# Keys kept once in the first stage, and experts' rows scattered straight to their tokens: one core of Trainium2

## The reference, cut to what matters

```
x = x + xattn0(layernorm(x), ctx)      # layer 0: 8 batches x 16 heads, 256 queries, 1601 keys, d_c = 64
x = x + ffn0(layernorm(x))             # 64 chosen tokens of each batch
x = x + xattn1(layernorm(x), ctx)      # layer 1: causal, 16 heads of 16
x = x + moe(layernorm(x))              # the last stage:
  xt = x.reshape(2048, 256); probs = softmax(xt @ Wg)          # 8 experts
  eidx = argmax(probs); gate = probs[eidx]
  pos = rank of the token among those of its expert; keep = pos < 256
  xd[eidx * 256 + pos] = xt, where keep                        # dispatch, 8 x 256 slots
  oe = (silu(xd @ W1) * (xd @ W3)) @ W2                        # per expert, hidden 352
  out = oe[eidx * 256 + pos] * gate * keep
  result = out + (silu(xt @ sw1) * (xt @ sw3)) @ sw2           # shared expert on every token
```

## Time and profile before

| what | us |
|---|---|
| median of 3 runs (lowest, highest) | 1929.41 (1920.93, 1934.65) |
| the profiled execution's own time | 1930.45 |
| its span in the trace | 1928.6 |
| busy in the span: PE, DVE, ACT, POOL | 1681.5, 1360.5, 1021.9, 959.9 |

### The profile page before, as it was taken

How to read it: one execution, slowest core, us unless ns; L and a number is a source line. 1 busy time by engine, 2 the same in 40 slices (tenths; PEclk the granted TensorE clock), 3 DMA queues, 4 the chain that set the end, 5 groups by cost and what they waited for, 6 DMA issues and landing times. The chain is left out here.

```text
span 1928.6 us, 48966 instructions
## 1 busy us (share of the span) xinstructions
PE 1681.5 (87%) x16216; PEld 1335.3 (69%) x16216; DVE 1360.5 (71%) x2953; ACT 1021.9 (53%) x2038; POOL 959.9 (50%) x623
## 2 busy tenths in 40 slices
PE   7316999999999999999999999979588777859687
PEld 5214888888888888888888888868464344438576
DVE  6885888888888888888888888866644555553113
ACT  5223666666666666666666666622122556542121
POOL 3741777777777777777777777720001211112103
PEclk8556999999999999999999999989798899988899
DMA  9412112112122122121121141274100000012254
GB/s 270 149 35 66 49 56 84 53 56 85 53 62 76 49 82 62 50 93 48 56 84 53 56 151 53 62 242 154 50 9 26 12 12 11 5 59 89 94 159 128
DMA packets 154184, 146.61 MB, mean 76 GB/s; under 512 B 41856, under 2 KB 141740, under 8 KB 153632
## 3 DMA queue, kind: packets, MB, share of 16 engines
q1 hardware_dynamic: 146464, 136.47, 23.4%
q10 hardware_dynamic: 6144, 5.54, 0.9%
q0 software_dynamic: 1536, 4.08, 0.7%
HBM read 94.67 MB, written 31.85 MB: 66 GB/s over the span
## 5 line engine op out<-in xcount | busy, mean ns | idle before, releaser
L1076 POOL TENSOR_TENSOR c_rest<-c_prob 128x1024 f16<-128x1024 f32 (+1 forms) x513 | 796.6, 1574 | 335.7 <-ACT c_prob L915 323.1
L995 DVE TENSOR_REDUCE c_mxp<-c_psM 128x1 f32<-128x400 f32 (+1 forms) x1040 | 589.2, 573 | 114.3 <-PE c_psM L776 99.7
L915 ACT ACTIVATE c_prob<-c_psS,ln,c_exp_scale 128x1024 f32<-128x1024 f32 (+1 forms) x514 | 536.7, 1044 | 240.4 <-PE c_psS L792 235.3
L792 PE MATMUL c_psS<-c_q,c_kk 128*128 128x256 f16 (+1 forms) x3350 | 512.7, 272 | 1.7 <-ACT c_prob L915 1.6
L810 PE MATMUL c_psV<-c_vb,c_prob 128*128 128x129 f16 (+1 forms) x3328 | 396.5, 222 | 0.5 <-POOL c_rest L1076 0.5
L792 PEld LDWEIGHTS c_psS<-c_q,c_kk 128*128 128x128 f16 (+1 forms) x3350 | 321.8, 99 | 87.7 <-ACT c_prob L915 2.3
L813 PE MATMUL c_psV<-c_vb,c_rest 128*128 128x65 f16 (+1 forms) x3328 | 374.2, 193 | 0.0
L776 PE MATMUL c_psM<-c_kkm,c_q 128*128 128x400 f16 (+1 forms) x1040 | 348.1, 335 | 5.9 <-DVE c_mxp L995 3.6
L813 PEld LDWEIGHTS c_psV<-c_vb,c_rest 128*128 128x128 f16 (+1 forms) x3328 | 301.4, 99 | 22.1
L810 PEld LDWEIGHTS c_psV<-c_vb,c_prob 128*128 128x128 bf16 (+1 forms) x3328 | 305.4, 97 | 15.0 <-POOL c_rest L1076 0.7
L738 PE MATMUL c_psQ<-c_xb,c_w2s 128*128 128x256 f16 x1188 | 164.9, 276 | 4.9 <-DVE c_roped L963 2.5
(11 more groups left out here) (296 smaller groups left out, 2219.6 us busy)
## 6 DMA issues: line engine op xcount, KB each, us to landing
c_w2s<-w_scr SPq DMA_DIRECT2D x67, 256.0 KB, 2.6
acc_scr<-c_acc SPq DMA_DIRECT2D x128, 129.0 KB, 2.1
c_ms<-m_scr SPq DMA_DIRECT2D x67, 192.0 KB, 2.3
c_w2s<-w_scr SPq DMA_DIRECT2D x67, 128.0 KB, 2.0
kv<-acc_scr SPq DMA_DIRECT2D x4, 2064.0 KB, 9.9
d_acc<-acc_scr SPq DMA_DIRECT2D x4, 2064.0 KB, 8.2
m_w<-in_L_ffn_W SPq DMA_DIRECT2D x20, 352.0 KB
c_kk<-KK SPq DMA_DIRECT2D x48, 128.0 KB, 2.0
```

The costliest lines, as they stand in the source:

```text
L792: mm = pe.matmul(psS[g % 2][0:r, i * S:(i + 1) * S], src[:, (lo + i) * P:(lo + i) * P + r], mov[slot][:, :], start=(one == 0 and i % 2 == ...
L915: nc.scalar.activation(prob[g][0:r, 0:w], psS[g % 2][0:r, 0:w], ACT.Exp, bias=keep["ln1024"][0:r, :], scale=exp_scale[slot][0:r, :]).then_ ...
L995: nc.vector.tensor_reduce(mxp[:, st, c:c + 1], psM[:, st, 0:CHUNKS[c][1]], AX.X, ALU.max).then_inc(mx_done, 1)
L1076: nc.gpsimd.tensor_tensor(rest[g][0:r, 0:w], prob[g][0:r, 0:w], high[0:r, 0:w], ALU.subtract).then_inc(rest_done, 1)
```

## The change

1. `KK2` is gone. The tile `kk2` of the attention stage takes its upper 64 partitions from `KK1` by DMA, and POOL fills its lower 64 once, at the start of the attention stage. The twelve DMAs for batch 0 are issued by SP instead of ACT, after its three DMAs for the second pair of heads.
2. A dispatched row is two words longer (`RW` = 258): behind the 256 elements of `xn` stand the token's number and its gate. All 8 experts' rows are loaded by 8 DMAs right after the scatters, into one tile; `HEAD` is 6 instead of 4.
3. DVE multiplies an expert's output with the gate as it leaves PSUM (`weigh`), and POOL scatters it at once to the token's row of `routed_scr`, which was filled with zeros. After the last expert SP loads that whole array in four DMAs, and DVE adds it in four instructions of 128 x 1024. `g_idx`, `oe_scr` and the gathers are gone. The loops over experts on PE and DVE are written out.

```diff
-            pool.wait_ge(aall_ready, 1)
-            nc.gpsimd.memset(KK2[0:2 * SHIFT_ROWS, :], SHIFT_ONE).then_inc(filled, 1)
-            pool.wait_ge(filled, 1)
-            nc.gpsimd.memset(KK2[2 * SHIFT_ROWS:DC, :], 0.0).then_inc(filled, 1)
-            pool.wait_ge(filled, 2)
...
-            def copy_high(b):
-                dve.wait_ge(k1_done, 2 * b + 2)
-                nc.vector.tensor_copy(KK2[DC:P, b * L:(b + 1) * L], KK1[DC:P, b * L:(b + 1) * L]
-                                      ).then_inc(high_copied, 1)
...
-                if b % 2 == 0 and b > 0:
-                    copy_high(b - 1)
-            copy_high(B - 1)
...
-                if b % 2 == 0:
-                    nc.scalar.activation(KK2[DC:P, b * L + lo * P:b * L + lo * P + w], ps[n % 8][DC:P, 0:w],
-                                         ACT.Copy).then_inc(k2_done, 1)
...
-        for part, whole in ((kk1, KK1), (kk2, KK2)):
-            queue.dma_start(part[:, c0:c1], whole[:, bass.ds(b * L + c0, c1 - c0)]).then_inc(in_kk[g], 16)
+        for part, rows in ((kk1, slice(0, P)), (kk2, slice(DC, P))):
+            queue.dma_start(part[rows, c0:c1], KK1[rows, bass.ds(b * L + c0, c1 - c0)]).then_inc(in_kk[g], 16)
...
+                if p == 0:
+                    for g in range(4):
+                        refill_scores(sp, 0, g)
+                    for g in range(4):
+                        refill_values(sp, 0, g)
...
+            pe.wait_ge(filled, 2)
...
-            for g in range(4):
-                refill_scores(act, 0, g)
-            for g in range(4):
-                refill_values(act, 0, g)
...
+            nc.gpsimd.memset(kk2[0:2 * SHIFT_ROWS, :], SHIFT_ONE).then_inc(filled, 1)
+            nc.gpsimd.memset(kk2[2 * SHIFT_ROWS:DC, :], 0.0).then_inc(filled, 1)
...
+RW = D + 2
...
+    row_ids, row_gates = rows[:].bitcast(U32)[:, :, D:D + 1], rows[:, :, D + 1:D + 2]
...
-    xd = [sb(f"xd{i}", [P, 2, D]) for i in range(2)]
+    xd = sb("xd", [P, E1, 2, RW])
...
-    HEAD = NS // 2
+    HEAD = 3 * NS // 4
...
-            sp.wait_ge(zeroed, 1)
+            sp.wait_ge(emptied, 2)
             for k in range(4):
                 sp.dma_start(t["xd_scr"].rearrange("(k p r) d -> k p (r d)", k=4, p=P)[k],
-                             zero[:]).then_inc(in_z, 16)
+                             empty[:].rearrange("p r d -> p (r d)")).then_inc(in_z, 16)
...
+            sp.wait_ge(zeroed, 1)
+            for k in range(4):
+                sp.dma_start(t["routed_scr"].rearrange("(k p r) d -> k p (r d)", k=4, p=P)[k],
+                             zero[:]).then_inc(in_z, 16)
...
-                sp.dma_start(xd[u][:], t["xd_scr"][u * CAP1:(u + 1) * CAP1, :].rearrange("(c p) d -> p c d", p=P)
-                             ).then_inc(in_xd[u], 16)
-            with sp.Fori(0, E1 // 2) as j:
+            for e in range(E1):
+                sp.dma_start(xd[:, e], t["xd_scr"][e * CAP1:(e + 1) * CAP1, :].rearrange("(c p) d -> p c d", p=P)
+                             ).then_inc(in_xd[e], 16)
+            with sp.Fori(0, E1 // 2 - 1) as j:
                 for u in range(2):
                     e = 2 * j + u
                     sp.wait_ge(y_full, 2 * (HEAD + e) + 2)
-                    weights((e + 2) % E1, u)
-                    sp.dma_start(xd[u][:], t["xd_scr"][bass.ds(((e + 2) % E1) * CAP1, CAP1), :]
-                                 .rearrange("(c p) d -> p c d", p=P)).then_inc(in_xd[u], 16)
-                    sp.wait_ge(y_done, 2 * (HEAD + e) + 4)
-                    sp.dma_start(t["oe_scr"][bass.ds(e * CAP1, CAP1), :].rearrange("(c p) d -> p c d", p=P),
-                                 yo[u][:]).then_inc(stored[u], 16)
+                    weights(e + 2, u)
...
-                sp.wait_ge(in_w[u], 64 * (E1 // 2 + 1))
-                sp.wait_ge(in_xd[u], 16 * (E1 // 2 + 1))
-                sp.wait_ge(stored[u], 16 + 16 * (E1 // 2))
-            for j in range(NT // 4):
-                sp.wait_ge(x_final, 4 * j + 4)
-                sp.dma_start(t["out"].rearrange("b (s p) d -> p (b s) d", p=P)[:, 4 * j:4 * j + 4, :],
-                             x[:, 4 * j:4 * j + 4, :]).then_inc(out_sent, 16)
-            sp.wait_ge(out_sent, 16 * (NT // 4))
+                sp.wait_ge(sent[u], 32 * (E1 // 2))
+            for k in range(4):
+                rows_k = slice(k * NT // 4, (k + 1) * NT // 4)
+                sp.dma_start(back[:, rows_k, :],
+                             t["routed_scr"].rearrange("(j p) d -> p j d", p=P)[:, rows_k, :]).then_inc(in_back[k], 16)
+            for k in range(4):
+                rows_k = slice(k * NT // 4, (k + 1) * NT // 4)
+                sp.wait_ge(x_final, k + 1)
+                sp.dma_start(t["out"].rearrange("b (s p) d -> p (b s) d", p=P)[:, rows_k, :],
+                             x[:, rows_k, :]).then_inc(out_sent, 16)
+            for u in range(2):
+                sp.wait_ge(in_w[u], 64 * (E1 // 2))
+            sp.wait_ge(out_sent, 64)
...
-            for u in range(2):
-                pool.wait_ge(stored[u], 16 + 16 * (E1 // 2))
-            for j in range(NT):
-                nc.gpsimd.indirect_dma_start(
-                    out=back[:, j, :], out_offset=None, in_=t["oe_scr"],
-                    in_offset=bass.IndirectOffsetOnAxis(ap=g_idx[:, j:j + 1], axis=0),
-                    bounds_check=E1 * CAP1 - 1, oob_is_err=False).then_inc(gathered, 16)
-            pool.wait_ge(gathered, 16 * NT)
+            for e in range(E1):
+                for r in range(2):
+                    pool.wait_ge(y_done, 2 * (HEAD + e) + r + 3)
+                    nc.gpsimd.indirect_dma_start(
+                        out=t["routed_scr"],
+                        out_offset=bass.IndirectOffsetOnAxis(ap=xd[:].bitcast(U32)[:, e, r, D:D + 1], axis=0),
+                        in_=yo[e % 2][:, r, :], in_offset=None, bounds_check=B * S - 1, oob_is_err=False
+                    ).then_inc(sent[e % 2], 16)
...
-            with pe.Fori(0, E1 // 2 - 1) as j:
-                own(2 * j + 1, j, 1, (HEAD + 2 * j, w2[0], 0))
-                own(2 * j + 2, j + 1, 0, (HEAD + 2 * j + 1, w2[1], 1))
-            own(E1 - 1, E1 // 2 - 1, 1, (HEAD + E1 - 2, w2[0], 0))
+            for e in range(1, E1):
+                own(e, e // 2, e % 2, (HEAD + e - 1, w2[(e - 1) % 2], (e - 1) % 2))
...
-            def copy_out(e, j, u):
-                for r in range(2):
-                    if r == 0:
-                        act.wait_ge(stored[u], 16 * j + 16)
-                    act.wait_ge(y_full, 2 * (HEAD + e) + r + 1)
-                    nc.scalar.activation(yo[u][:, r, :], psY[r][:, 0:D], ACT.Copy).then_inc(y_done, 1)
...
+            def weigh(e):
+                for r in range(2):
+                    if r == 0 and e >= 2:
+                        dve.wait_ge(sent[e % 2], 32 * (e // 2))
+                    dve.wait_ge(y_full, 2 * (HEAD + e) + r + 1)
+                    nc.vector.tensor_scalar(yo[e % 2][:, r, :], psY[r][:, 0:D], xd[:, e, r, D + 1:D + 2], None,
+                                            ALU.mult).then_inc(y_done, 1)
...
-            link(nc.vector.tensor_copy(g_idx[:], slot[:]))
-            link(nc.vector.tensor_tensor(gate[:], gate[:], keepm[:], ALU.mult))
...
-            with dve.Fori(0, E1 // 2) as j:
-                for u in range(2):
-                    gated(HEAD + 2 * j + u, u)
...
-                for j in range(j0, j1):
-                    nc.vector.scalar_tensor_tensor(out=x[:, j, :], in0=back[:, j, :], scalar=gate[:, j:j + 1],
-                                                   in1=x[:, j, :], op0=ALU.mult, op1=ALU.add).then_inc(x_final, 1)
+            for e in range(E1):
+                if e > 0:
+                    weigh(e - 1)
+                gated(HEAD + e, e % 2)
...
+                if k == 0:
+                    weigh(E1 - 1)
...
-            dve.wait_ge(gathered, 16 * NT)
             dve.wait_ge(y_done, 2 * n + 2)
-            add_own(0, NT - 4)
-            add_shared(n, i)
-            dve.wait_ge(y_done, 2 * n + 4)
-            add_own(NT - 4, NT)
+            for k in range(4):
+                rows_k = slice(k * NT // 4, (k + 1) * NT // 4)
+                if k == 3:
+                    add_shared(n, i)
+                    dve.wait_ge(y_done, 2 * n + 4)
+                dve.wait_ge(in_back[k], 16)
+                nc.vector.tensor_tensor(x[:, rows_k, :], x[:, rows_k, :], back[:, rows_k, :],
+                                        ALU.add).then_inc(x_final, 1)
```

More of the change, by code:

```diff
@@ L555, in phase_attention0 @@
     AHEAD = 4
-    V, KK1, KK2, xh, xl = keep["V"], keep["KK1"], keep["KK2"], keep["xh"], keep["xl"]
+    V, KK1, xh, xl = keep["V"], keep["KK1"], keep["xh"], keep["xl"]
     kk1 = sb("c_kk1", [P, L], F16)
@@ L2004, with phase_moe @@
 CAP1 = B * S // E1
+RW = D + 2
 FT1 = [(0, 128), (128, 128), (256, 96)]
-def phase_moe(nc, ctx, t, x, xn, xT):
+def phase_moe(nc, ctx, t, x, rows, xT):
     def sb(name, shape, dt=F32):
@@ L2016, in phase_moe @@
     FTN = len(FT1)
```

(46 more changed lines are left out.)

41 lines of the change are left out of this document (21 added, 20 removed).

## The result

| | before | after |
|---|---|---|
| median of 4 runs each (lowest, highest), us | 1927.92 (1920.93, 1934.65) | 1879.15 (1866.66, 1881.89) |
| the profiled execution's time, its span | 1930.45, 1928.6 | 1879.77, 1877.9 |
| ratio, 95% interval | | 0.9744 (0.9698 to 0.9789) |

The changed kernel is 2.6% faster; the forecast was 1883.

The account below looks back on a forecast made before the run. Bounds: PE's chain of waits in the experts' stage, a DVE, PE, ACT chain in the keys'. 1930.45 - 17.5 + 0.3 - 29.2 = 1884.1 profiled, median 1.0 lower: 1883; range 1874 to 1890, with three rivals 1871 to 1898.

Parts of the forecast that it names:

- part 1: Keys and values: without the second copy of the keys 17.5 us gained, DVE no longer held by POOL's memset.
- The start of the attention: Attention's start: POOL's memset of `kk2` costs 0 to 2.7 us, taken as 0.3; SP's key DMAs have 8 us of cover.
- The long window: Loop over the heads of layer 0, 1378 of 1928.6 us: counted at no change.
- T0: Experts' stage: time at which the first expert's step begins, predicted 1801.1, including 2.9 us for a late silu.
- Rival (a): Experts' stage: late signals grow beside the scatter burst, T0 is 1808.6 and the time 1890.5; chance 0.10.
- The steps: Experts' stage: 9.04 us per expert, 72.3 for eight, where it was 10.6 each.
- Rival (c): Expert steps: weights take the place of the rows, steps stay at 10.6 us, time 1895.5; chance 0.09.
- Rival (b): Scatters ahead of the experts: longer rows cost POOL double, 2.6 us each, time 1897; chance 0.08.
- Rival (d): Expert steps: each pair of POOL's scatters holds PE's signals 7 us, time 1939, slower than before; chance 0.03.
- Rival (e): `kk2`'s keys or a scatter are late, so PE or SP waits: single us, in the range; no chance of its own.
- The tail: After the eight experts: shared tiles, loads, additions and output end at T0 + 98.3 = 1899.4, 29.2 us gained.

Follow-up runs that it names:

- e1_keys_only: Changed kernel with the whole experts' stage of the kernel before put back; 1910.44 us, ratio 0.9898 to the kernel before.
- e6_memsets_kept: Changed kernel with POOL's two long first-stage memsets back, on a tile that nothing reads; 1902.62 us, ratio 0.9852 to the kernel before.
- e4_rows_behind_weights: Changed kernel with dispatched rows from the third expert on loaded behind that expert's weights again; 1899.59 us, ratio 0.9838 to the kernel before.
- e2: Kernel before with six instead of four shared tiles ahead of the experts, nothing else; 1939.87 us, ratio 1.005.
- e3: Kernel before with six shared tiles first and all dispatched rows loaded at once, results still stored and gathered; 1931.18 us, ratio 1.0007.
- e8: Changed kernel where `down` waits for the product's last third only ahead of the matmul reading it; 1887.69 us, ratio 0.9782 to the kernel before.
- e13: The kernel of e8 once more, without pauses, on the chip of e12; 1884.38 us, ratio 0.9758 to the kernel before.
- e12: Changed kernel with the later wait of e8 and two POOL pauses in the burst of scatters; 1876.18 us, ratio 0.9723 to the kernel before.
- e5: Changed kernel with four instead of six shared tiles ahead of the experts; 1896.18 us, ratio 0.9823 to the kernel before.
- e7: The kernel before, unchanged, profiled once more on a second chip; 1929.83 us, one profile.

## Why the prediction was right, point by point

**The keys' copy held to 0.1 us.** `e1_keys_only` and `e6_memsets_kept` show it apart: 10.2 us for the memset that held DVE (9.98 in part 1), 7.2 for the copies and their waits (6.9).

**The start of the attention.** I took 0.3 us for POOL's memset; DVE isn't held at all. The Trainium skill (SBUF — State Buffer, Who interferes with whom) has it so for DVE instructions with at most one SBUF input outside the two-port modes, and the trace agrees: POOL's 1.43 us and DVE's 0.64 us lie side by side. Of the measured -1.4, 1.2 are luck: PE's first matmuls ran at the higher clock in this profile, and not in the second one of the same kernel. PE's busy time before doesn't tell the cases apart: in the 6 us ahead of the seam it was 3.5 us both here (granted clock 0.62, then 1.47 us for the twelve matmuls) and in `e4_rows_behind_weights` (0.50, then 2.72).

**The long window.** I called 1378 us the loop over the heads of layer 0. It holds the stages behind that loop too, up to well into layer 1. The forecast doesn't suffer, since none of them was changed and the window stayed the same to 1 us.

**T0.** I counted 2.9 us for a late signal, carried over from the earlier trace rows. In the changed kernel the signal isn't late; that is the whole miss of 2.7. That was luck: in six other profiles with six shared tiles ahead (e2, e3, e4, e6, e8, e13) signals were late, and T0 came 9.2 to 12.9 us later than without. Rival (a) had it at 1808.6 - 1798.2 = 10.4 by the same count, so its mechanism and its size are those of these runs. Had the changed kernel been among the six, its time would have been 1889 to 1893, near the 1890.5 of (a). Some late signal, of one burst or the other, is in every program here without pauses but the changed one, so a chance of 0.10 was too low.

**The steps.** 9.04 predicted, 8.97 measured, and 8.46 for the first. Waits for rows had made the 10.6 of before: `e4_rows_behind_weights` gives them back, 10.9 us of waiting. Rival (c), that weights would take the place of the rows, falls: PE waits for no weights in any of these runs.

**The scatters.** Rival (b) falls at 1.30 us per scatter. Rival (d), late signals with every expert, falls: with two scatters per 9 us no instruction of ACT or DVE waits for a `remote` signal anywhere in the changed kernel's experts' stage. `e3_no_row_scatter` prices this part at some 19 us. Rival (e) falls too: PE waits for no `kk`, and DVE's last additions for no load.

**The tail.** T0 to the end was 97.0, and I had 98.3: 1.0 too much in the steps, and 0.8 in the additions, which take 1.21 to 1.23 us and start 1.13 apart where I took 1.33; the output's last DMA took 0.5 more.

The individual values of `HEAD`, rows and scatters don't stand alone: `HEAD` brings at most 4.9 us by itself and 13.9 with the others in place, and in the run of `HEAD` alone the stall turned it into a loss.

## What to carry to other kernels

Find what a tiny instruction waits for when its duration is absurd for its size: here 10 us hung on a memset of another tile on another engine. Where a queue brings two things of which one is needed first, load the early-known one ahead for all rounds; and where the results are sent to their final rows as they come, the tail has only plain additions left. Where many indirect DMAs follow each other on POOL, look at the idle time of ACT and DVE in the second half of the burst, and try a pause that waits for what has been sent: two pauses cost under 1 us here and took away a stall of 8 to 11 (e12 against e13 and e8).

## What the runs showed of the hardware that was not expected

**Signals of PE come late behind a long run of indirect DMAs.** In the six profiles in which PE stood still the scatters start 1.3 us apart without a pause, the lateness begins 10 to 12 us after the first, and the last held signal goes through 0.9 to 2.6 us after the last scatter's end. PE's matmuls run on meanwhile, as far as their waits let them. With four shared tiles ahead (before, e1, e5, e7) a signal is late too (ACT idles 3.2 to 6.7 us until it comes), but it goes through before the last scatter ends, and PE waits for the rows anyway. Bursts of six, five and five with 2.3 to 2.5 us between them didn't show it in two profiles, nor do pairs.

That pauses remove it rests on `e12_late_wait_pauses` against `e13_late_wait_again` and `e8_late_wait`, one kernel on one chip; its five times with pauses (1875.5 to 1877.6) lie below all six of e8 and four of the five of e13. Since the changed kernel, with 16 scatters in a row, is spared on two chips while the same experts' stage behind another first stage (`e6_memsets_kept`) is not, it isn't excluded that another small change of the program would do the same. What is held, and why, stays open. Instruction loads lie within the first 8 us of the burst, in stalled and spared kernels alike, so nothing here makes them the cause.

**A memset of POOL holds one DVE instruction and not another.** The f32 instruction of one input on 128x16 stands for 10.24 us, the f32 to f16 ones of 128x832 and DVE's own memsets not at all. `e6_memsets_kept` shows that the memset does it, on whatever tile; what sets the held instruction apart (its type, its size or its form) no run tests.
